# Padding the transposed row maxima to 128 columns and issuing one score part ahead of the outputs

## The reference

```
x = x + 0.5 * ffn(layernorm(x))
x = x + attention(layernorm(x))
x = x + 0.5 * ffn(layernorm(x))
```

## Time and profile before

| | |
|---|---|
| median of 3 runs | 596.79 us |
| profiled execution | 597.72 us |
| its span | 595.9 us |
| TensorE matmul busy (PE) | 562.6 us, 94% |
| VectorE busy (DVE) | 484.8 us, 81% |
| ScalarE busy (ACT) | 396.6 us, 67% |
| GpSimd busy (POOL) | 167.5 us, 28% |
| TensorE's granted clock | 0.997 of full |

### The profile page before, as it was taken

The page is one execution under the profiler, slowest core; times in us unless marked ns, Lnnn a source line. Parts: engine busy times, 40 slices in busy tenths (PEclk is TensorE's granted clock), DMA queues, the critical chain, the costliest instruction groups (busy, mean ns, idle before and its releaser), DMA issues.

```text
span 595.9 us, 12386 instructions
## 1 busy us (share of the span) xinstructions
PE 562.6 (94%) x4244; PEld 344.3 (58%) x4244; DVE 484.8 (81%) x1865; ACT 396.6 (67%) x713; POOL 167.5 (28%) x262
## 2 busy tenths in 40 slices
PE   2869999999999989999999999998999999999998
PEld 2335565555566756666566666554446656665666
DVE  6998988999876889898989897986797688756654
ACT  4647656665645458797878878886667755764642
POOL 3024201101430034454545454656401101101100
PEclk9999999999999999999999999998999999999999
DMA  8701001101204251424233233211101112211112
GB/s 314 223 19 36 19 19 36 36 7 31 37 4 115 40 133 46 101 60 90 74 76 100 65 83 84 66 50 39 37 1 36 54 54 54 54 54 54 35 36 72
DMA packets 72222, 37.90 MB, mean 64 GB/s; under 512 B 35520, under 2 KB 71616, under 8 KB 72128
## 3 DMA queue, kind: packets, MB, share of 16 engines
q1 hardware_dynamic: 72160, 37.11, 23.9%
HBM read 18.22 MB, written 10.49 MB: 48 GB/s over the span
## 4 chain that ended last, share of the span: by engine, by line
PE 72%; DVE 17%; DMA 3%; ACT 3%; issue 2%; POOL 2%; SPq 1%; DVEq 0%; ACTq 0%; POOLq 0%
PE bank L1126 33%; PE bank L1138 17%; DVE sm_out L960 7%; PE bank L1225 5%; PE bank L1282 4%; PE bank L1293 4%; PE bank L1252 4%; PE bank L1307 2%; PE bank L1298 2%; DMA q_st<-mx_hl 2%; DVE hid L823 1%; DVE hl L838 1%; PE bank L1117 1%; DVE stats L702 1%; POOL xn L403 1%
## 5 line engine op out<-in xcount | busy, mean ns | idle before, releaser
L960 DVE CUSTOM_DVE_ANT_0 sm_out<-bank,mask 128x256 f16<-128x256 f32 (+1 forms) x512 | 151.3, 352 | 18.7 <-PE bank L1252 18.0
L464 ACT ACTIVATE silu<-bank,w_scale 128x512 f32<-128x512 f32 x128 | 87.2, 682 | 116.2 <-PE bank L1126 114.9
L823 DVE SCALAR_TENSOR_TENSOR hid<-silu,h_unit,bank 128x512 f32<-128x512 f32 x128 | 95.0, 743 | 62.6 <-ACT silu L464 62.1
L1138 PE MATMUL bank<-wT_down,hh 128*128 128x256 f16 x512 | 118.2, 273 | 1.8 <-DVE hl L838 1.6
L1138 PE MATMUL bank<-wT_down,hl 128*128 128x256 f16 x512 | 118.2, 273 | 0.0
L1126 PE MATMUL bank<-xh,wT_gate 128*128 128x512 f16 x256 | 97.4, 381 | 4.4 <-DVE hid L823 4.4
L1126 PE MATMUL bank<-xh,wT_up 128*128 128x512 f16 x256 | 98.0, 383 | 1.2 <-DVE xl L767 1.2
L838 DVE TENSOR_TENSOR hl<-hid,hh 128x512 f16<-128x512 f32 x128 | 98.2, 768 | 0.0
L1126 PE MATMUL bank<-xl,wT_up 128*128 128x512 f16 x256 | 98.0, 383 | 0.0
L1126 PE MATMUL bank<-xl,wT_gate 128*128 128x512 f16 x256 | 97.3, 380 | 0.0
L412 POOL TENSOR_TENSOR xnl<-xn,xnh 128x1024 f16<-128x1024 f32 x13 | 27.7, 2130 | 238.0 <-ACT xn L501 180.4
(11 more groups left out here) (131 smaller groups left out, 790.6 us busy)
## 6 DMA issues: line engine op xcount, KB each, us to landing
q_st<-q_scratch SPq DMA_DIRECT2D x32, 256.0 KB
q_scratch<-q_hl SPq DMA_DIRECT2D x16, 256.0 KB, 2.3
out_dram<-x SPq DMA_DIRECT2D x7, 512.0 KB, 3.0
x<-in_x_dram SPq DMA_DIRECT2D x1, 3072.0 KB, 15.5
k_scratch<-k_hl SPq DMA_DIRECT2D x16, 128.0 KB, 2.4
k_st<-k_scratch SPq DMA_DIRECT2D x16, 128.0 KB
x<-in_x_dram SPq DMA_DIRECT2D x2, 512.0 KB, 4.6
shared<-in_w_up_t_dram SPq DMA_DIRECT2D x2, 512.0 KB, 6.5
```

What stands on the lines that cost most here:

```text
L464: act.activation(silu[:, e % 2, :], U[e % 2][:, :], ACT.Silu, scale=w_scale[:, 0:1]).then_inc(silu_ready, 1)
L823: dve.scalar_tensor_tensor(out=hid[:, e % 4, :], in0=silu[:, e % 2, :], scalar=h_unit[:, 0:1], in1=GT[e % 2][:, :], op0=ALU.mult, op1=ALU. ...
L960: ins = dve.tensor_tensor_reduce(sm_out[:, i, cols], SM[i][:, cols], mask[:, S - size:S], -1.0 / MAX_UNIT, -MASKED, ALU.add, ALU.min, rowm ...
L1138: ins = pe.matmul(ACC[t % 2][:, 0:D], part[:, par, e, t * P:(t + 1) * P], wT_down[:, e, :], start=(e == 0 and part is hh), stop=(e == NE - ...
```

## The change

Two things change. First, `mx_q` grows from 32 to 128 columns for each half: the 32 columns with the parts are as before (`mx_parts`), the other 96 are zeroed once at the start by GpSimd, and the transpose takes all 128, so that it fills 128 rows of PSUM. ScalarE still copies 32 rows. Second, score part 0 of the odd groups 3 to 61 is issued by TensorE one iteration earlier in the code: right ahead of the outputs of groups n-1 and n it issues part 0 of group n+2, which it otherwise issued in the next iteration, after row-max part 0. These are 30 matmuls. The other engines' lists are as before, except for the one memset on GpSimd.

```diff
--- before.py
+++ after.py
@@ -121,7 +121,8 @@
         rowmax = sb("rowmax", [P, 2, QT, H])
         sm_out = sb("sm_out", [P, 3, 2 * S], F16)
         ident16 = sb("ident16", [P, P], F16)
-        mx_q = sb("mx_q", [P, 2, 2, HH, QT], F16)
+        mx_q = sb("mx_q", [P, 2, P], F16)
+        mx_parts = mx_q[:, :, 0:2 * HH * QT].rearrange("p n (a h t) -> p n a h t", a=2, h=HH)
         mx_hl = sb("mx_hl", [2 * QT * HH, 2, P], F16)
         o_rec = sb("o_rec", [P, 2, H])
         o_norm = sb("o_norm", [P, 2, D])
@@ -131,8 +132,8 @@
         U, GT, ACC, TR = bank[0:2], bank[2:4], bank[4:6], bank[6:8]
         SM, ST, PV, MI = bank[0:3], bank[3:5], bank[5], bank[6:8]
         LAST_ST = [SM[1], ST[0], ST[1]]
-        MT = PV[0:2 * QT * HH, 0:P // 2].bitcast(F16)
-        FIRST_MT = ST[0][0:2 * QT * HH, 0:P // 2].bitcast(F16)
+        MT = PV[:, 0:P // 2].bitcast(F16)
+        FIRST_MT = ST[0][:, 0:P // 2].bitcast(F16)
 
 
         ld_w = [[sem(f"ld_w{m}{half}") for half in range(2)] for m in range(3)]
@@ -196,6 +197,10 @@
         def score_bank(n, i):
 
             return LAST_ST[i] if n >= NG - G else ST[(3 * n + i) % 2]
+
+        def begun_early(n):
+
+            return 2 < n < NG - 2 and n % 2 == 1
 
         def copied_by_vector(n):
 
@@ -339,6 +344,7 @@
             step(pool.affine_select(out=ident32[:, :], in_=ident32[:, :], compare_op=ALU.not_equal, fill=1.0,
                                     base=0, pattern=[[-1, P]], channel_multiplier=1))
             step(pool.tensor_copy(ident16[:, :], ident32[:, :]))
+            step(pool.memset(mx_q[:, :, :].bitcast(U32), 0))
             pool.memset(ones[:, :], 1.0).then_inc(const_ready, 1)
             pool.wait_ge(const_ready, 1)
             step(pool.memset(k_st[64:P, :, :, :].bitcast(U32), 0))
@@ -366,9 +372,9 @@
                 if b:
                     pool.wait_ge(mxT_ready, 2 * b + half - 1)
                 heads = rowmax[:, b % 2, :, half * HH:(half + 1) * HH].rearrange("p t h -> p h t")
-                pool.tensor_copy(mx_q[:, half, 0, :, :], heads).then_inc(mxhi_ready, 1)
+                pool.tensor_copy(mx_parts[:, half, 0, :, :], heads).then_inc(mxhi_ready, 1)
                 pool.wait_ge(mxhi_ready, 2 * b + half + 1)
-                pool.tensor_tensor(mx_q[:, half, 1, :, :], heads, mx_q[:, half, 0, :, :],
+                pool.tensor_tensor(mx_parts[:, half, 1, :, :], heads, mx_parts[:, half, 0, :, :],
                                    ALU.subtract).then_inc(mxlo_ready, 1)
 
             def attention_pair(pair, last):
@@ -562,7 +568,7 @@
                 if not (isinstance(b, int) and b == 0):
                     act.wait_ge(mx_loaded[half], 32 * b)
                 maxima = FIRST_MT if b + half == 0 else MT
-                act.activation(mx_hl[:, half, :], maxima, ACT.Copy).then_inc(mx_ready, 1)
+                act.activation(mx_hl[:, half, :], maxima[0:2 * QT * HH, :], ACT.Copy).then_inc(mx_ready, 1)
 
             def exps(n, parts):
 
@@ -1259,7 +1265,7 @@
                 pe.wait_ge(mxlo_ready, 2 * b + half + 1)
                 if b + half:
                     pe.wait_ge(mx_ready, 2 * b + half)
-                pe.transpose(MT if b + half else FIRST_MT, mx_q[:, half, :, :, :].rearrange("p a h t -> p (a h t)"),
+                pe.transpose(MT if b + half else FIRST_MT, mx_q[:, half, :],
                              ident16[:, :]).then_inc(mxT_ready, 1)
 
             def scores(n, b, k, g, parts=range(3)):
@@ -1326,6 +1332,7 @@
                                 project(c + 2, at // 4, at % 4)
 
 
+                        second = (n + 2, b + (g + 2) // 4, k + (g + 2) // 4, (g + 2) % 4)
                         following = (n + 1, b + (g + 1) // 4, k + (g + 1) // 4, (g + 1) % 4)
                         if ahead:
                             if g == 2:
@@ -1334,7 +1341,7 @@
                             if odd or g:
                                 max_scores(*lead, range(0, 1))
                         projection(0)
-                        if not (end and g == 3):
+                        if not (end and g == 3) and not begun_early(n + 1):
                             scores(*following, range(0, 1))
                         if g % 2 and not end:
                             pe.wait_ge(oT_ready, n)
@@ -1372,6 +1379,8 @@
                             outputs((n,), k)
                         elif g % 2:
                             pe.wait_ge(mx_ready, 2 * (b + 1) + g // 2 + 1)
+                            if begun_early(n + 2):
+                                scores(*second, range(0, 1))
                             outputs((n - 1, n), k)
                         if odd and g == 3 and not last:
                             val_transposes(c + 2, (onorm_ready, 2 * b + 1))
```

## The result

The changed kernel takes 611.99 us (median, 611.49 to 612.98), the kernel before 596.51 us beside it: the ratio is 1.0246 (95% interval 1.0228 to 1.0263), 15.5 us slower. The forecast was 607.4 us, in a range of 601 to 612. The direction and the mechanism were right; the size was a third short (15.5 us where 10.6 were forecast), and the measured time lies 0.01 us inside the range's upper end. That it lies inside is luck.

The account below looks back on a forecast made before the run. The prediction took TensorE to set the pace in attention. Six stretches with projections (+9.9 us), the last two (+1.1) and the first two transposes (-0.4) gave +10.6 us on 596.79: 607.4 us, range 601 to 612.

Parts of the forecast that it names:

- place 1: First of four outputs passes in a two-batch stretch: moved score's wait delays the outputs by +0.10 us, at least -0.19.
- place 2: Second outputs pass of a stretch, where ScalarE runs late: outputs delayed by +0.45 us, between +0.20 and +0.65.
- place 3: Third outputs pass of a stretch: moved score waits 1.27 us for part 1's exponential, outputs delayed by +1.08 us.
- place 4: Fourth outputs pass: cycle becomes 5.62 us, +0.42 in one kind of stretch, -0.38 where TensorE had waited for VectorE.
- last two stretches: Stretches without projections to fill TensorE: two cycles +0.84 us, a third +0.5, the rest -0.2, in all +1.1.
- first two transposes: Padded transposes with no moved score behind them: they keep their gain, -0.4 us.
- the transposes' saving: Padded transposes in attention: score to next matmul 0.47 to 0.28 us, the 0.19 saved lost inside the moved scores' waits.
- The memset: Zeroing the padded tile on GpSimd at the start: costed at nothing, since ScalarE idles 5.40 us until the weights land.
- from exponential to score: On TensorE at each moved score: a score waiting for its bank starts 0.73 us after that exponential's start.
- A gap taken out of its stream is a gain: Attention phase: TensorE sets the pace, so removing a gap from its instruction stream saves time.
- rival 1: Moved score is free and only the transposes count: 32 x 0.19 = 6.1 us off, 590.7 us; chance 5%.
- Rival 2: Moved scores wait, but TensorE gets the time back from later waits that go: about +0, 597 us; chance 6%.

Follow-up runs that it names:

- third experiment: Changed kernel with the same 30 score parts issued right behind the outputs, not ahead of them: 596.77 us, ratio 1.0004 against the kernel before.
- fifth: Changed kernel with ScalarE's query parts put behind the exponential of part 1, not ahead of it: 606.84 us, ratio 1.0163 against the kernel before.
- sixth: Changed kernel with padded transposes and, of the 30 moved scores, only the 7 at place 3: 600.44 us, ratio 1.0055 against the kernel before.
- second: Changed kernel with the 32-column maxima of before, so only the moved scores: 612.57 us, ratio 1.0251 against the kernel before.
- fourth experiment: Changed kernel with TensorE's wait for the maxima copy behind the moved score, not ahead: 610.02 us, ratio 1.0213 against the kernel before.
- eighth: Kernel with padding and only group 61's score moved; even groups' first score also put ahead of row-max part 0: 597.46 us, ratio 1.0004.
- ninth: Kernel with padding and only group 61's score moved; even groups' first score ahead of row-max part 0 in odd batches only: 594.46 us, ratio 0.9952.

## Why the prediction was right, and what was short

Up to the outputs of group 59 the profile of the changed kernel is 15.45 us behind that of before. By the prediction's own terms, in us (each place once, then over the six stretches with projections):

| term | forecast | measured | forecast, six stretches | measured, six stretches |
|---|---|---|---|---|
| place 1 | +0.10 | +0.29 | 0.6 | 1.7 |
| place 2 | +0.45 | +0.53 | 2.7 | 3.2 |
| place 3 | +1.08 | +1.14 | 6.5 | 6.8 |
| place 4, the two kinds | +0.42, -0.38 | +0.59, -0.20 to -0.40 | 0.1 | 1.0 |
| last two stretches | +1.1 | +2.7 | | |
| first two transposes | -0.4 | not seen | | |

**Right.** The moved score waits for its bank's exponential, the chain to it is first score, first exponential, maxima copy, query part (places 2 and 3), second exponential, and everything behind it on TensorE waits with it. The third experiment takes the wait away and nearly all of the loss with it; the fifth shortens one link by 0.57 us and the cycles follow one for one; the sixth shows the wait and the loss at place 3 by itself. That VectorE's waits at place 4 pay part of it back was right too (sixth), and so was the transposes' saving being lost inside the waits (second). The memset, put at nothing, shows nothing: the first transpose starts at 204.2 us, before at 204.5.

**Mis-sized: from exponential to score.** I took 0.73 us from a score in the stream. The moved one needs 0.81, and the outputs follow it 0.30 behind where I took 0.32. Over the 29 moved scores that wait for their bank that is some 1.8 us of the 4.9 missing. At places 2 to 4 it comes from the wait instruction ahead of the score, which I had not counted (fourth experiment); at place 1 that is not the cause, and it stays open.

**Mis-sized: place 4.** I put the next group's first exponential 0.57 us behind the odd group's third, at ScalarE's pace. It stands 0.66 behind, since its own score comes 0.67 us behind the third one on TensorE:

```profile
359.01 0.39 PE L1288 MATMUL bank<-q_st,k_st 128*128 128x512 f16 x1
359.24 0.38 PE L1258 MATMUL bank<-k_st,q_st 128*128 128x256 f16 x2
359.68 0.38 PE L1288 MATMUL bank<-q_st,k_st 128*128 128x512 f16 x1
```

That is 0.09 of the 0.18 us by which the cycle, 5.80 us, exceeds my 5.62, at nine places; most of the other half is the exponential-to-score time.

**Mis-sized: the last two stretches.** I put their edges at -0.2 us because TensorE waited there already. The cycles at both edges to place 1 came out 0.61 us longer, and the three between them 1.95 us longer together where I had 1.34 (0.18 each, as at place 4); the one to the outputs of group 59 came out 0.48 shorter. Together that is the 2.7. Twice the transpose waits there, 1.4 us in all, for GpSimd's parts of the row maxima (the list above). GpSimd's timeline at the first of the two:

```profile
395.77 1.41 POOL L401 TENSOR_TENSOR x<-x,o_norm 128x256 f32<-128x256 f32 x2 [2.09 <-DVE o_norm L982]
397.13 0.20 POOL L375 CAST mx_q<-rowmax 128x16 f16<-128x16 f32 x1
397.41 0.22 POOL L377 TENSOR_TENSOR mx_q<-rowmax,mx_q 128x16 f16<-128x16 f32 x1
```

The parts (L375, L377) stand behind the additions of the outputs (L401), which wait 2.09 us for VectorE's normalisation, and that follows the outputs of place 4. Later outputs make the next transpose late, a loop that I had not looked for. This is read from the trace and was not tested.

**Mis-sized: place 1.** Of the missing 0.19 us, 0.06 are the exponential-to-score time and the outputs behind it. The other 0.13 lie between the outputs of place 4 and that exponential; the transposes of the normalised tiles described at the third experiment (1.00 us where it was 0.88) fit them, which is read and not tested.

**Wrong, without weight in the sum.** "A gap taken out of its stream is a gain": the padding alone should then have given 6.1 us, by rival 1. It gave 1.7. TensorE was busy nearly throughout, but at three of four places something else held it from the same moment on: at place 3, and in three stretches at place 4, the exponential that the third score waits for; in the other three at place 4 VectorE; at place 1 the xT copies. For place 3 the eighth and ninth experiments confirm it, since an earlier first score shortens that cycle by 0.24 us; the others are read from the profiles. I had the numbers for place 3 in the earlier trace rows: the third score stood at 345.41, and 344.67 + 0.73 = 345.40. I never made that comparison. It is also why TensorE reached the moved score 1.38 us after the first one and not 1.19. So rival 1 had the wrong price, 590.7, where the padding alone took 595.8 and the same scores behind the outputs 596.8. Rival 2's price was wrong too: its own terms (2.4 and 3.2 us less in the stretches, 3.1 less in the last two) take 10.6 to +1.9, 598.7, and not to 597.

The padded load takes 96 ns in the changed kernel, the 32-column one took 92 ns. The rule of the Trainium skill that the load time goes with the number of columns ("TensorE: Matmul & The Clock Gate", section "LDWEIGHTS (loading the stationary operand)") is not borne out here.

Between the outputs of group 59 and the end the changed kernel gains 1.2 us. Windows of the kernel before and of the changed one, at the outputs of group 59:

```profile
414.00:417.00 3.00, 2.86 (x33) 1.67 (x34) 0.00 (x0) 0.79 (x2) 1.22 (x2) 0.55 0.02 3
```

```profile
430.00:433.00 3.00, 2.44 (x40) 1.35 (x34) 0.69 (x1) 1.74 (x4) 1.58 (x3) 1.00 0.02 3
```

In the profile before, TensorE was granted 0.55 of its clock there (most of the time the lower level, 1.2 GHz), after some 6 us with several waits (4.36 us busy from 408 to 414); those outputs took 2.69 us where they take 1.44 in the changed kernel's profile at the full 2.4 GHz. That is no work of the change: the profile of the move alone has the lower level at these outputs too (0.50 from 429.5 to 432.5), and that of the padding alone keeps 1.00, after a like time with less work in it (4.05 us busy from 406.5 to 412.5). What decides it is not shown here. So the span difference (14.2 us) is smaller than that of the medians (15.5).

## What to carry to other kernels

Before an instruction is put forward on a busy in-order engine, compute when its operand or buffer is free, not whether its work fits: here 0.22 us of unchanged work, put ahead of a pass it does not belong to, waited at 29 of 30 places, up to 1.16 us, with everything behind it. And "this engine is busy 97% of the stretch" does not say that shortening its stream helps: check at each place whether the next instruction's other condition came within the time that you hope to save, since a chain that ends at the same moment shows no wait until the first one is shortened.

## What was not expected of the hardware

Two waits in a row on one queue are not always free even when the first is long fulfilled: at places 2 to 4 the second's score started 0.81 us after the exponential with the other wait ahead of it, and 0.72 without, 1.6 us over 21 places. At place 1 it was 0.81 both ways. And a stationary operand of 32 columns costs TensorE about 0.2 us around it (0.47 against 0.27 us from score to next matmul), though its load is no longer than a full one. The Trainium skill ("TensorEngine Tiling (Array Packing)", section "Key Properties") says that a change of the tiling mode drains the engine; the gap that went with the padding agrees.
